# Dealing the contraction axis to tiles as 512c + 4p + 2r + h: longer rows and pairs of tiles per load

## The reference

```python
x = x + einsum(einsum(x, B0[ids]), A0[ids])                  # rank 16, adapter by request
base   = einsum('btd,od->bto', x, W)
logits = einsum('btd,ed->bte', x, Wr) + 5.0 * one_hot(language)
gates  = softmax over the two largest logits
h      = einsum('btd,erd->bter', x, A)
x = x + base + 2.0 * einsum('bter,bte,eor->bto', h, gates, B)
```

## Time and profile before

| | |
|---|---|
| median of 3 runs | 1563.22 us (1560.31 to 1563.93) |
| the profiled execution | 1561.31 us, of which the span of its instructions is 1559.5 us |
| PE busy | 1541.5 us, 99% |
| DVE busy | 1230.4 us, 79% |
| ACT busy | 714.2 us, 46% |
| HBM | 278.52 MB read, 66.72 MB written |

### The profile page before, as it was taken

One profiled execution on the slowest core, in us unless ns is written; L12 is line 12 of the kernel. 1 busy time (PEld: TensorE's weight loads), 2 busy tenths in 40 slices (PEclk: granted clock), 3 DMA queues, 4 the chain that ended last, 5 costly groups with the idle time before them and its releaser, 6 DMA issues.

```text
span 1559.5 us, 20275 instructions
## 1 busy us (share of the span) xinstructions
PE 1541.5 (99%) x7430; PEld 1298.3 (83%) x7430; DVE 1230.4 (79%) x1692; ACT 714.2 (46%) x911; POOL 79.7 (5%) x119
## 2 busy tenths in 40 slices
PE   9989999999999999999999999999999999999998
PEld 8778878888888888888888888888888888888887
DVE  6998878977799767887688776997769976787665
ACT  6522222544445444455445444454444554445442
POOL 2333331000000000000000000000000000000000
PEclk9999999999999999999999999999999999999999
DMA  9899999787777767687676977667776777666564
GB/s 263 224 276 281 265 254 246 215 230 205 218 231 220 216 196 231 219 229 220 203 224 196 257 207 218 216 205 231 209 218 226 215 217 195 214 219 217 198 219 160
DMA packets 303109, 347.04 MB, mean 223 GB/s; under 512 B 204890, under 2 KB 236682, under 8 KB 302346
## 3 DMA queue, kind: packets, MB, share of 16 engines
q1 hardware_dynamic: 293602, 314.28, 69.8%
q0 software_dynamic: 9136, 30.94, 6.0%
q10 hardware_dynamic: 272, 0.52, 0.1%
HBM read 278.52 MB, written 66.72 MB: 221 GB/s over the span
## 4 chain that ended last, share of the span: by engine, by line
PE 88%; DVE 5%; SPq 4%; DMA 2%; issue 1%; ACT 0%; DVEq 0%; ACTq 0%
PE pb L804 26%; PE pb L805 26%; PE pb L806 26%; PE pb L378 4%; PE pb L380 3%; PE pb L533 2%; SPq L669 2%; SPq L292 2%; DVE raw L684 1%; DVE xl L558 1%; DMA out_dram<-ost 1%; DVE pool_a L540 1%; DMA raw<-in_L_cond_W_dram 0%; DMA an<-in_L_cond_A_dram 0%; PE pb L319 0%
## 5 line engine op out<-in xcount | busy, mean ns | idle before, releaser
L796 ACT CAST wh<-raw 128x1024 fp32r<-128x1024 f32 (+1 forms) x453 | 475.4, 1049 | 705.3 <-PE pb L806 670.9
L800 DVE TENSOR_TENSOR wl<-raw,wh 128x1024 fp32r<-128x1024 f32 (+1 forms) x453 | 552.1, 1219 | 261.3 <-ACT wh L796 260.0
L804 PE MATMUL pb<-wh,sh 128*128 128x512 f32 x1568 | 612.8, 391 | 0.5 <-DVE ost L858 0.5
L805 PE MATMUL pb<-wl,sh 128*128 128x512 f32 x1568 | 611.6, 390 | 0.0
L806 PE MATMUL pb<-wh,sl 128*128 128x512 f32 x1568 | 611.2, 390 | 0.0
L806 PEld LDWEIGHTS pb<-wh,sl 128*128 128x128 f32 x1568 | 294.3, 188 | 62.8
L804 PEld LDWEIGHTS pb<-wh,sh 128*128 128x128 f32 x1568 | 294.5, 188 | 56.2 <-DVE wl L800 0.9
L805 PEld LDWEIGHTS pb<-wl,sh 128*128 128x128 f32 x1568 | 294.6, 188 | 55.1
L378 PE MATMUL pb<-awb,xah 128*128 128x304 f32 x512 | 139.0, 305 | 0.3 <-DVE xal L355 0.3
L380 PE MATMUL pb<-awb,xal 128*128 128x256 f32 x512 | 134.6, 280 | 0.0
L804 PE MATMUL pb<-wh,xh 128*128 128x512 f32 x256 | 101.5, 396 | 0.8 <-DVE xl L558 0.8
(11 more groups left out here) (153 smaller groups left out, 1258.6 us busy)
## 6 DMA issues: line engine op xcount, KB each, us to landing
raw<-t_scr SPq DMA_DIRECT2D x392, 512.0 KB, 4.1
xst<-in_x_dram SPq DMA_DIRECT2D x448, 64.0 KB, 3.8
out_dram<-ost SPq DMA_DIRECT2D x72, 256.0 KB, 3.5
raw<-in_L_cond_W_dram SPq DMA_DIRECT2D x124, 128.0 KB, 5.3
raw<-bt_scr SPq DMA_DIRECT2D x28, 512.0 KB, 3.6
out_dram<-u SPq DMA_DIRECT2D x56, 256.0 KB, 2.9
t_scr<-raw POOLq DMA_DIRECT2D x32, 256.0 KB, 4.4
t_scr<-tst POOLq DMA_DIRECT2D x16, 512.0 KB, 6.7
```

Of the source, the lines that this page charges most:

```text
L796: e.copy(pair_split(wh, g), pair_source(g)).then_inc(c_wh, 1)
L800: e.tensor_tensor(out=pair_split(wl, g), in0=pair_source(g), in1=pair_split(wh, g).bitcast(f32), op=ALU.subtract).then_inc(c_wl, 1)
L804: e.matmul(o, h, wh[:, g % RING, k, :], start=start, stop=False)
L805: e.matmul(o, h, wl[:, g % RING, k, :], start=False, stop=False)
```

## The change

Index d = 512c + 4p + 2r + h of the contraction axis now goes to partition p of a tile that is named by c, r and h; before it was d = 256k + 2p + h. So rows of 128 elements (512 bytes) are read, and a load of W (`unit_load`) brings half of the output columns of two pairs of tiles; the two units 2m and 2m+1 together hold the pairs 2m and 2m+1. A turn needs both units of its pair and reads every fourth word of each.

- W's loads have three places (two of `raw`, one of `xst`); x of batch 1 has one place where it had two. Units 2 and 3 go to `xst2`.
- Blocks of x are loaded in four DMAs of 128 KB instead of eight of 64 KB, in all batches.
- Turns of W with an odd number stand ahead of `adapt` and `pair_lo` in their slot; for x of batch 1 two halves are turned in every second slot, ahead of that.
- The gated part's rows have their own loads (`gated_load`); the columns of B0 are turned in two instructions instead of one; the views of the start (`tile_of`, `x_transpose`, `a0_transpose`, `a0_copy`) follow the new dealing; a wait was added in `first_hi`.

The diff, shortened:

```diff
@@ -249,16 +250,23 @@
-        x_b = x.rearrange("b (h v j) (c k a n) -> b h c k a j v n", h=2, j=32, c=4, k=2, a=4)
-
-        def x_block(m):
-            return xst[:, m % 2, :, :].rearrange("p t n -> p (t n)")
+        x_b = x.rearrange("b (h v j) (c a n) -> b h c a j v n", h=2, j=32, c=4, a=4)
+
+        def x_block(n, m):
+            return xst[:, m % 2 if n > 1 else 0, :, :].rearrange("p t n -> p (t n)")
+        def wait_x(e, n, m):
+            if n == 1:
+                e.wait_ge(d_x[0], 64 * (m + 1))
+            else:
+                e.wait_ge(d_x[m % 2], (0 if m % 2 else 512) + 64 * (4 * (n - 2) + m // 2 + 1))
         def x_turn(e, n, u):
             q, kp = x_unit(u)
             m = u // 2
             if u % 2 == 0:
-                e.wait_ge(d_x[m % 2], 128 * (4 * (n - 1) + m // 2 + 1))
+                wait_x(e, n, m)
             if kp == 0:
                 b = n - 1
                 if n == 1:
...
@@ -274,24 +282,29 @@
-            e.transpose(two(n, q, kp).rearrange("p (g j) -> p g j", g=16),
-                        x_block(m).rearrange("p (g i h) -> p h g i", g=16, h=2)[:, u % 2, :, :]).then_inc(c_xc, 1)
+            e.transpose(two(n, q, kp).rearrange("p (r v j) -> p r v j", r=2, v=8),
+                        x_block(n, m).rearrange("p (v i r h) -> p h r v i", v=8, r=2, h=2)[:, u % 2, :, :, :])\
+             .then_inc(c_xc, 1)
-            if n == 1 and m < 2:
-                if 0 in parts:
+            if n and 0 in parts:
+                if n == 1 and m == 0:
-            elif n and 0 in parts:
-                e.wait_ge(c_xc, 16 * (n - 1) + 2 * m - 2)
+                elif n == 1:
+                    e.wait_ge(c_xc, 2 * m)
+                elif n == 2 and m == 0:
+                    e.wait_ge(c_xc, 16)
+                elif n == 2 and m == 1:
+                    e.wait_ge(c_wc, 64)
+                else:
+                    e.wait_ge(c_xc, 16 * (n - 1) + 2 * m - 2)
-                    for k in range(2):
-                        e.dma_start(x_block(m)[32 * a:32 * a + 32, k * CW:(k + 1) * CW]
-                                    .rearrange("p (v n) -> p v n", v=8), x_b[n, half, cols, k, a])\
-                         .then_inc(d_x[m % 2], 16)
+                    e.dma_start(x_block(n, m)[32 * a:32 * a + 32, :].rearrange("p (v n) -> p v n", v=8),
+                                x_b[n, half, cols, a]).then_inc(d_x[m % 2 if n > 1 else 0], 16)
...
@@ -315,7 +328,7 @@
                 wait_kept(e, 0, u - 2)
             for k in range(2):
                 for t in range(2):
-                    block = x_place(m)[:, t, :].rearrange("p (k n h) -> p k h n", k=2, h=2)[:, k, u % 2, :]
+                    block = x_place(m)[:, t, :].rearrange("p (n k h) -> p k h n", k=2, h=2)[:, k, u % 2, :]
                     last = e.transpose(pb[:, x_bank(u), (2 * k + t) * P:(2 * k + t + 1) * P], block, ident[:, :])
             last.then_inc(c_tr, 1)
...
@@ -550,6 +563,8 @@
             if u == 8:
                 e.wait_ge(d_ar, 48)
                 e.wait_ge(d_as, 32)
+            if u == 12:
+                e.wait_ge(c_wc, 8)
             e.copy(xh0[:, 2 * kp:2 * kp + 2, q, :], quarter(0, q)[:, 2 * kp:2 * kp + 2, :]).then_inc(c_h0, 1)
         def first_lo(e, u):
...
@@ -617,57 +632,55 @@
...
+        def unit_place(n):
+            if n in (2, 3):
+                return xst2[:, n - 2, :, :].rearrange("p t n -> p (t n)")
+            at = n if n < 2 else (n - 1) % 3
+            return (raw[:, at, :, :] if at < 2 else xst[:, 1, :, :]).rearrange("p t n -> p (t n)")
+        def unit_landed(e, n):
+            if n in (2, 3):
+                e.wait_ge(d_w2, 128)
+            elif n < 2:
+                e.wait_ge(d_w[n], 64)
+            else:
+                at = (n - 1) % 3
+                e.wait_ge(d_w[at], 64 * ((n - 1) // 3 + (at < 2)))
+
+        raw_w = W.rearrange("(c w g j) (q a n) -> c w q a j g n", c=4, w=2, j=32, q=4, a=4)
+        def unit_load(e, n):
+            if n in (2, 3):
+                e.wait_ge(c_tr, 16)
+            elif n == 6:
+                e.wait_ge(c_bt, 4)
+            elif n in (4, 5):
+                e.wait_ge(c_wc, 4)
+            elif n > 6:
+                e.wait_ge(c_wc, 4 * ((n - 3) // 2) + 4)
+            landed = d_w2 if n in (2, 3) else d_w[n] if n < 2 else d_w[(n - 1) % 3]
+            for a in range(4):
+                e.dma_start(unit_place(n)[32 * a:32 * a + 32, :].rearrange("p (g n) -> p g n", g=8),
+                            raw_w[n // 8, n % 2, n // 2 % 4, a]).then_inc(landed, 16)
+        def gated_place(c):
+            return btx[:, :] if c < 3 else raw[:, 1, 0, :]
+        def gated_load(e, c):
+            if c == 1:
+            elif c == 2:
+            else:
+                e.wait_ge(c_wc, 60)
+            for w in range(2):
+                e.dma_start(gated_place(c)[:, w * HT:(w + 1) * HT], bt_scr[:, w, c * HT:(c + 1) * HT]).then_inc(d_btx, 16)
...
@@ -675,19 +688,20 @@
             c, k = divmod(g, 9)
             w = w_number(g)
             diagonal = k // 2 == c
-            raw_landed(e, g)
+            for n in range(w // 2 * 2, w // 2 * 2 + 2):
+                unit_landed(e, n)
             if w >= 2:
                 e.wait_ge(c_wl, g - 2 - (g % 9 < 2) + 1)
                 wait_sums(e, w - 2)
                 e.wait_ge(d_bs[w % 2], 32 * (w // 2))
-            for h in range(2):
-                e.transpose(w_kept(g)[:, h, :].rearrange("p (g j) -> p g j", g=16),
-                            w_raw(g).rearrange("p (g i h) -> p h g i", g=16, h=2)[:, h, :, :])\
+            for n in range(2):
+                e.transpose(w_kept(g)[:, :, n * HT:(n + 1) * HT].rearrange("p h (g j) -> p h g j", g=8),
+                            unit_place(w // 2 * 2 + n).rearrange("p (g i r h) -> p r h g i", g=8, r=2, h=2)[:, k % 2, :, :, :])\
                  .then_inc(c_id if diagonal else c_wc, 1)
             if diagonal:
+                e.wait_ge(c_id, 4 * c + 2 * (k % 2) + 2)
                 for h in range(2):
-                    e.wait_ge(c_id, 4 * c + 2 * (k % 2) + h + 1)
-                    block = w_kept(g)[:, h, k % 2 * HT:(k % 2 + 1) * HT].rearrange("p (n h) -> p h n", h=2)[:, h, :]
+                    block = w_kept(g)[:, h, :].rearrange("p (n s) -> p s n", s=4)[:, k % 2 * 2 + h, :]
                     e.tensor_tensor(out=block, in0=block, in1=ident[:, :], op=ALU.add).then_inc(c_wc, 1)
...
@@ -1012,22 +1026,24 @@
-                e.wait_ge(c_bt0, n - 1)
+                e.wait_ge(c_bt0, 2 * (n - 1))
-                e.dma_start(columns_place(n)[32 * a:32 * a + R, 0:CW].rearrange("p (k n) -> p k n", k=HK),
-                            B0[bass.ds(adapter[n], 1), :, :].rearrange("b r (k a n) -> a (b r) k n", k=HK, a=4)[a])\
+                e.dma_start(columns_place(n)[32 * a:32 * a + R, 0:CW].rearrange("p (c n) -> p c n", c=4),
+                            B0[bass.ds(adapter[n], 1), :, :].rearrange("b r (c a n) -> a (b r) c n", c=4, a=4)[a])\
-            e.transpose(columns_place(n)[:, CW:2 * CW].rearrange("p (h k j) -> p h k j", h=2, k=HK),
-                        columns_place(n)[:, 0:CW].rearrange("p (k i h) -> p h k i", k=HK, h=2)).then_inc(c_bt0, 1)
+            for h in range(2):
+                e.transpose(columns_place(n)[:, CW:2 * CW].rearrange("p (h c r j) -> p h c r j", h=2, c=4, r=2)[:, h, :, :, :],
+                            columns_place(n)[:, 0:CW].rearrange("p (c i r h) -> p h c r i", c=4, r=2, h=2)[:, h, :, :, :])\
+                 .then_inc(c_bt0, 1)
-            e.wait_ge(c_bt0, n)
+            e.wait_ge(c_bt0, 2 * n)
...
@@ -1047,7 +1063,7 @@
         def tile_of(t, n):
-            return t.rearrange("p (k n h) -> p h k n", k=HK, h=2)[:, n // HK, n % HK, :]
+            return t.rearrange("p (c n r h) -> p h c r n", c=4, r=2, h=2)[:, n // HK, n % HK // 2, n % 2, :]
         def a_tiles(m):
             return slice(m % 2 * HK + m // 2 * 4, m % 2 * HK + m // 2 * 4 + 4)
...
@@ -1104,15 +1120,15 @@
             if g >= 6:
                 e.wait_ge(c_al, g - 5)
             for m in range(4):
-                at = 4 * (g % 4) + m
+                at = 4 * m + g if g < 4 else 4 * (g - 4) + m
                 block = a0p[:, at, :, :].rearrange("p b r -> p (b r)") if g < 4 else a0t[:, at * P:(at + 1) * P]
                 last = e.transpose(pb[:, a0_bank(g), m * P:(m + 1) * P], block, ident[:, :])
             last.then_inc(c_at, 1)
         def a0_copy(e, g):
             e.wait_ge(c_at, g + 1)
-            e.copy(a0t[:, :].rearrange("c (h p s) -> c s h p", h=2, s=HK)[:, 2 * g:2 * g + 2, :, :],
-                   pb[:, a0_bank(g), :].rearrange("c (s h p) -> c s h p", s=2, h=2)).then_inc(c_ac, 1)
+            e.copy(a0t[:, :].rearrange("n (h c r q s) -> n h r s c q", h=2, c=4, r=2, s=4)[:, g % 2, g // 2, :, :, :],
+                   pb[:, a0_bank(g), :].rearrange("n (s c q) -> n s c q", s=4, c=4)).then_inc(c_ac, 1)
         def a0_hi(e, g):
             e.wait_ge(c_at, 4 + g + 1)
...
@@ -1378,18 +1398,20 @@
```

(63 more changed lines are left out.)

24 lines of the change are left out of this document (2 added, 22 removed).

## The result

The changed kernel takes 1603.79 us (median of 4 runs, 1603.31 to 1606.37), the kernel before on the same chip 1561.76 (1559.85 to 1563.93): a ratio of 1.0272, 95% interval 1.0252 to 1.0292, or 42 us more. The sign is as forecast, the size is not: 1581 was predicted, 1592 was the upper end of the range.

The account below looks back on a forecast made before the run. PE was taken as bound by its own work after 275 us, by DVE's before. Rows -2.9, turns +2.0, +7.0 and +6, PE's loads +6 made +18 on 1561.3; with 1.9 to the median, 1581 us, range 1557 to 1592.

Parts of the forecast that it names:

- the upper end of the range: Whole kernel: 1592 us, leaving out the forecast's worst, 1593 (turns 18 us, PE's loads +12, low clock 3.4, less 2.9).
- What bounds the kernel: PE bound by its own work after 275 us, by DVE's before; a better schedule alone could give back 18 us.
- The turns: DVE in batch 0: every fourth word costs +0.5 us a turn; +2.0 before the `a0g` DMA, +7.0 to slot 7, +6 after.
- The third of its terms: DVE, 109 to 200 us: 42 turns at +0.5 us make 96.7 us of work in 91 us, +6 us.
- the stretch for which the prediction had 0: DVE, 200 to 270 us: 16 turns at +0.5 us add 8 to 56.9 of 70 us; it fits, 0.
- PE's weight loads: Start on PE, 7.9 to 33 us: 88 loads at every fourth word, each 0.067 us longer, +6 us; bounds 0 and 12.
- Longer rows: SP's queue, slots 9 to 24: half the x DMAs free 3.5 us per two slots; -2.9 us, -4.2 at best.
- the late output DMA at 231 us: Batch 0: output DMA issued late, DVE's copy behind it stalls PE 2.6 us; freeing SP's queue could remove this.
- Pairs of units and x's single place: DVE's waits for second units and x's next block, batch 0: bounds 0 and +8 us; 0 taken if turns are slow.
- Rival B: Strides are free, but pairs and x's single place make DVE wait, +3 to +8 us: 1563 to 1568; chance 0.13.
- a second such stretch: PE at the low clock, 1.2 GHz, once more after a stall: 3.4 us, counted only in the worst case, 1593.

Follow-up runs that it names:

- The table: Eight versions of the changed kernel: every second or fourth word, one unit or two, x first or behind W; -1.3 to +42.0 us against the kernel before.

## Why the prediction was wrong

**What bounds the kernel: right.** Nothing was lost after batch 0, and slot 7 and the stretches behind it are where most of PE's new idle time lies.

**The turns: the mechanism was right before slot 7, the size a little high.** 0.5 us was taken, 0.38 measured. Up to slot 7 the sum had 18 turns; 18 x 0.38 is 6.8. Slot 7's first matmul, counted out in the timeline after, stands at

```profile
100.76 0.39 PE L818 MATMUL pb<-wh,xh 128*128 128x512 f32 x1
```

7.1 us behind the 93.62 of before, where 9 had been forecast. Alone in the kernel before the step is worth 12.4 us; the sum had 15 for DVE. The third of its terms was near by luck: at 0.38 us a turn, DVE's excess from 109 to 200 us would be 0.7 us and not 6. In the trace of the step alone, the transposition of the gated values in slot 7 begins 7.0 us late (107.91 for 100.92), the `delta` behind the stall of 231 us 8.8 us (243.19 for 234.36), and the other 2.8 of its 11.6 us come after that, in the stretch for which the prediction had 0. The upper end of the range was also added up too low: at 0.59 us a turn the third stretch alone gives 9.5 us and all three terms 20, not 18, so 1596. The result lies above that as well.

The Trainium skill, "SBUF — State Buffer", section "Door 1: The DMA port swizzle", asks for two hits in each line of 16 bytes. DVE's turns agree with it: with two words of a line 0.70 us, with one 1.08; so does the addition on the diagonal tiles, 0.27 and 0.38 us. Its words "4 fp32" for the step that is free are not borne out: a step of four floats is the one that costs.

**PE's weight loads: wrong, 6 us too much.** They feel the step from contiguous to every second word (140 to 207 ns) and nothing more from there to every fourth (207 ns). The prediction took the first increment once more, without a row for it.

**Longer rows: the amount about right, the place wrong.** -2.9 us were booked, most of it to the late output DMA at 231 us; long rows alone gave -1.7 and left that stall. In the changed kernel the stall before the same `delta` grew from 2.6 to 6.0 us, for a reason that is the next point.

**Pairs of units and x's single place: the failed step.** The prediction said: "If turns are slow, DVE arrives later than the loads and the price is 0, which I take for my forecast." The loads wait for the turns. SP issues the next units when the odd turn has ended, so when DVE comes to that turn later, the loads are later by the same amount. Only slow work between that turn and the next use could cover anything, one or two turns at 0.38 us, and it was not enough. The table shows it: these two waits cost 21.8 us with turns at every second word and 27.8 (42.0 - 14.2) with turns at every fourth. Around 258 us it can be read in full. The timelines of DVE and SP after:

```profile
257.40 1.05 DVE L698 STREAM_TRANSPOSE raw<-xst 128x512 f32<-128x512 f32 x1
...
265.95 2.04 DVE L698 STREAM_TRANSPOSE raw<-raw 128x512 f32<-128x512 f32 x2 [3.80 <-DMA raw<-in_L_cond_W_dram]
...
270.04 1.28 DVE L872 COPY ost<-pb 128x512 f32<-128x512 f32 x2
```

```profile
258.48 2.23 SPq L668 DMA_DIRECT2D raw<-in_L_cond_W_dram  x4
```

The odd turn ends at 258.45, at 258.48 the unit goes out, DVE waits for it until 265.95, and behind the turn in DVE's list stands the copy that frees PSUM for `delta`. That is the 6.0 us of L546.

**The size of the loop was off as well.** For x, the prediction had 12 issues of 0.7 us and 3.8 us to land, 12 us against a period of 13. Up to the last issue it took less, 5.7 and 6.3 us in the two rounds shown, but x landed 6.7 to 8.0 us after that issue began. 3.8 us was the median of all 448 of its DMAs in the whole kernel; between 118 and 175 us it is 4.7 in the kernel before, 6.6 in the changed one (with DMAs twice as large) and 4.3 in the changed one with x issued ahead of W. So much of the landing time comes from being issued behind the megabyte of W. And the turns that close the loop, of W and of x, were not in the 12 us at all. Measured, a round is 17.4 us with turns at every fourth word and 16.8 with turns at every second, above 13. Rival B had the mechanism and was given +3 to +8 us; with every second word it costs 20.5.

**What it adds up to.** The sum without PE's loads is -2.9 + 2 + 7 + 6 = 12 us, and long rows with the step measured 8. Of the 34 us that remain to 42, the wait for two units and x behind W, priced at 0, are 27.8; the other 6 (14.2 - 8.0) are slow turns in the new order of turns, which is hardly more than the uncertainty, and no run explains them; of the 3.9 us between the two traces, 2.8 are there when slot 7's transposition begins (109.44 and 106.62). A part of the 42 us is clock: PE's busy time grew by 14.6 us for the same instructions, as its granted clock fell to the lower level for some us about its new pauses (0.66 of full speed on average from 160 to 170 us, where a pause of 3.9 us ends at 163.18). The prediction had kept a second such stretch for the upper end only.

## What to carry to other kernels

A wait is not covered by a busy engine if that engine is what starts the transfer: before pricing it at nothing, follow the loop from the instruction that frees a place over the issue, the landing and the next use back to it, add up its turn, every issue ahead of it in the queue and the landing time with that queue's bytes in flight, and compare the sum with the period. Where each load holds parts for two uses, the first use waits for two loads; as many bytes in as many DMAs, needed one at a time, cost nothing here. And the median landing time on a page of the profile is that of its commonest surroundings, not of the place that you price.

## What the runs showed of the hardware

- DVE's 32 x 32 turns of 128 x 512 floats take 0.65 to 0.70 us at every second word and 1.03 to 1.08 us at every fourth; PE's load of 128 weights takes 140, 207 and 207 ns at every word, second and fourth; ACT's copy with its output at every fourth word took 1092 ns, at every eighth 1185 ns, contiguous 598 ns.
- DVE's addition of 128 x 128 floats in place took 0.27 us at every second word and 0.38 us at every fourth.
- Twice as long rows alone brought the packets from 303109 to 209411, the share of the busiest queue from 69.8% to 67.8% and the time down by 1.7 us.
- x's DMAs of 128 KB landed in 6.6 us (median, 118 to 175 us) in the changed kernel, where they are issued behind eight of 128 KB for W on the same queue, and in 4.3 us where they are issued ahead of these.
- DVE's `gate` operation took 3.11 us beside a GpSimd tensor_tensor of 2.35 us, and 0.19 us when that one was moved away.
